# Filter taps of a state-space convolution from powers and weights instead of one exponential per state

## The reference

```python
def _L0_attn_a_ref(u, A_log, D, C_re, C_im, log_dt):
    dt = jnp.exp(log_dt)                      # one per channel m, 128
    A = -jnp.exp(A_log)                       # one per state n, 64
    t = jnp.arange(L_, dtype=u.dtype)         # 256 samples
    at = dt[:, None, None] * A[None, None, :] * t[None, :, None]
    K = jnp.einsum('mn,mln->ml', C_re, jnp.exp(at))
    u_f = jnp.fft.rfft(u.transpose(0, 2, 1), n=2 * L_)
    k_f = jnp.fft.rfft(K, n=2 * L_)
    y = jnp.fft.irfft(u_f * k_f, n=2 * L_)[..., :L_]
    return y.transpose(0, 2, 1) + u * D
```

## Time and profile before

| | before |
|---|---|
| median of 3 runs | 856.48 us (856.13 to 857.97) |
| the profiled execution | 855.01 us, of which the span of the instructions is 853.3 us |
| PE busy | 801.8 us, 94% of the span |
| ACT busy | 719.8 us, 84% |
| DVE busy | 682.4 us, 80% |
| POOL busy | 550.3 us, 64% |

### The profile page before, as it was taken

How to read it: one execution, slowest core, us unless ns; L and a number is a source line. 1 busy time by engine, 2 the same in 40 slices (tenths; PEclk the granted TensorE clock), 3 DMA queues, 4 the chain that set the end, 5 groups by cost and what they waited for, 6 DMA issues and landing times.

```text
span 853.3 us, 20661 instructions
## 1 busy us (share of the span) xinstructions
PE 801.8 (94%) x7793; PEld 446.1 (52%) x7793; DVE 682.4 (80%) x2000; ACT 719.8 (84%) x919; POOL 550.3 (64%) x620
## 2 busy tenths in 40 slices
PE   5899898989999999999999999999999999999995
PEld 4644475666677623333333333333333677777774
DVE  6898699999998766777777777778736899888884
ACT  7640488778888899999999999999998889999984
POOL 1187455535553498988899888888887555454542
PEclk9999999999999999999999999999999999999998
DMA  8201100000003334343334433433420000000000
GB/s 263 69 1 49 50 2 1 2 2 2 2 1 77 95 70 98 87 86 89 100 101 100 100 96 90 97 87 91 98 41 2 1 14 15 14 14 14 14 14 17
DMA packets 38521, 46.20 MB, mean 54 GB/s; under 512 B 6696, under 2 KB 24368, under 8 KB 38416
## 3 DMA queue, kind: packets, MB, share of 16 engines
q1 hardware_dynamic: 38416, 44.83, 20.8%
HBM read 28.03 MB, written 16.78 MB: 53 GB/s over the span
## 4 chain that ended last, share of the span: by engine, by line
PE 61%; ACT 14%; DVE 13%; issue 9%; POOL 3%; SPq 0%; DMA 0%; ACTq 0%
PE psum L816 16%; PE psum L762 15%; PE psum L1114 12%; ACT prob L1072 11%; PE psum L1063 5%; PE psum L1172 4%; DVE mixed L828 3%; DVE normed L351 2%; PE psum L566 2%; POOL prob L1087 2%; ACT decay L420 1%; PE psum L956 1%; PE psum L533 1%; PE psum L637 1%; DVE hidden_parts_first L785 1%
## 5 line engine op out<-in xcount | busy, mean ns | idle before, releaser
L1072 ACT ACTIVATE prob<-psum 128x1536 f32<-128x1536 f32 x256 | 347.7, 1500 | 15.5 <-PE psum L1063 15.5
L1114 PE MATMUL psum<-prob,vstack 128*32 128x256 f32 (+1 forms) x2048 | 204.9, 495 | 1.6 <-DVE o_tok L1122 1.6
L762 PE MATMUL psum<-xt_parts,w_parts 128*128 128x512 f16 x768 | 186.6, 379 | 0.0
L828 DVE SCALAR_TENSOR_TENSOR mixed<-psum,comb_y,mixed 128x128 f32<-128x128 f32 x512 | 143.1, 339 | 2.1 <-PE psum L816 2.1
L792 POOL TENSOR_TENSOR hidden_parts_second<-hidden_second,hidden_parts_second 128x512 f16<-128x512 f32 x64 | 78.9, 1233 | 91.8 <-ACT hidden_parts_second L778 91.8
L792 POOL TENSOR_TENSOR hidden_parts_first<-hidden_first,hidden_parts_first 128x512 f16<-128x512 f32 x64 | 77.9, 1222 | 77.7 <-ACT hidden_parts_first L778 77.5
L776 ACT ACTIVATE hidden_first<-psum,b 128x512 f32<-128x512 f32 x128 | 88.3, 690 | 29.1 <-PE psum L762 22.0
L1082 POOL TENSOR_SCALAR_AFFINE_SELECT prob<-prob 128x512 f32<-128x512 f32 x128 | 82.4, 644 | 41.0 <-ACT prob L1072 35.5
L1063 PE MATMUL psum<-qstack,kstack 32*128 32x512 f16 x768 | 99.7, 385 | 9.7 <-POOL prob L1087 4.8
L1063 PEld LDWEIGHTS psum<-qstack,kstack 32*128 32x128 f16 x768 | 24.9, 91 | 158.2 <-ACT prob L1072 139.8
L816 PE MATMUL psum<-w_parts,hidden_parts_first 128*128 128x128 f16 x1536 | 96.0, 219 | 10.5 <-DVE mixed L828 5.7
(11 more groups left out here) (121 smaller groups left out, 1101.1 us busy)
## 6 DMA issues: line engine op xcount, KB each, us to landing
qstack<-qk_parts SPq DMA_DIRECT2D x128, 128.0 KB, 3.6
qk_parts<-parts SPq DMA_DIRECT2D x64, 192.0 KB, 3.2
kstack<-qk_parts SPq DMA_DIRECT2D x128, 32.0 KB, 3.5
stream<-L_attn_a_u SPq DMA_DIRECT2D x4, 512.0 KB, 8.4
kept_x<-stream SPq DMA_DIRECT2D x4, 512.0 KB, 2.6
out<-mixed SPq DMA_DIRECT2D x8, 256.0 KB, 2.3
w_whole<-L_ffn_W SPq DMA_DIRECT2D x1, 1024.0 KB, 7.6
taps<-c_taps SPq DMA_DIRECT2D x1, 640.0 KB, 9.8
```

The lines of the kernel that those rows point to most:

```text
L762: last = e.matmul(bank(u % 4), m.w1[:, w_part, ex, cols], xt_parts[:, s, x_part, :], start=(n == 0), stop=(n == len(PRODUCTS) - 1))
L828: last = e.scalar_tensor_tensor(out=m.y[:, t0 + t, :], in0=bank(down_bank(m, i))[:, t * P:(t + 1) * P], scalar=comb_y[:, s, t, ex:ex + 1], ...
L1072: e.activation(prob[:, n % PROBS, :], psum[:, TILE * (n % 2):TILE * (n % 2 + 1)], ACT.Exp, scale=SCALE)\
L1114: last = e.matmul(to[SLOT * lane:SLOT * (lane + 1)], vstack[:, b % 2, keys, first:first + SLOT], weights_of(n - t, lane, keys, pair), star ...
```

## The change

Each exponential is split as t = 64 q + l, with four quarters q and 64 samples l: exp(z t) = exp(z l) * exp(z 64 q). Partitions are now two channels by 64 states, and 64 columns are the other 64 pairs of channels, so that `z` has one value for each of 128x64.

- The host lays `C_re`, `log_dt`, `A_log` and a ramp of 64 samples into one array `tap_cols` of 128x193, one transfer in place of four. `eye` and `skip_d` come later in the queue; `taps`, `inverse` and the chunks of the stream come ahead of `w1` and `w2`. Each has its own semaphore.
- ACT: four exponentials of 128x64, `leap`, for the quarters; five in place over `powers`, two of 128x512 and three of 128x1024.
- DVE: `grid` writes z * l into `powers` (pieces 0, 1, 2 and 4, TENSOR_TENSOR), and two products of 64x256 make `weight`, `leap` times the column of `C_re`, zero in the half of the other channel. POOL sets `weight` to zero and writes piece 3 of `powers`.
- PE: 32 fp32 products with `powers` (128x128) stationary and `weight` (128x16) moving. Each contracts over the 64 states. Half of what each gives is of use: `ktap_move` copies it to `ktap`, two copies by DVE and two by ACT. DVE adds `skip_d` to the first tap's row.
- Order: on PE the forward transforms 0 and 1 of chunk 0 stand behind the tap products, 2 and 3 behind the transform of the taps. On DVE the statistics of chunk 1 now stand behind `skip_d`.

```diff
-        for n in range(STATES):
-            if n >= ERING and n % 2:
-                e.wait_ge(chained, (n - ERING) // 2 + 1)
-            elif n >= ERING:
-                e.wait_ge(tapped, (n - ERING) // 2 + 1)
-            e.activation(decay[:, n % ERING, :], ramp[:], ACT.Exp, scale=z[:, n:n + 1]).then_inc(decayed, 1)
-        e.wait_ge(tapped, STATES // 2 + 2)
-        for h in range(HALVES):
-            last = e.copy(ktap[:, h, :], bank(6 + h)[:, 0:P])
+        for q in range(QUARTERS):
+            last = e.activation(leap[:, q, :], z[:], ACT.Exp, scale=float(QUARTER * q))
+        last.then_inc(leaped, 1)
+        for i, (lo, hi) in enumerate(GRIDS):
+            if i == GPSIMD_GRID:
+                e.wait_ge(gridded_too, 1)
+            else:
+                e.wait_ge(gridded, i + (i < GPSIMD_GRID))
+            piece = powers[:, lo:hi, :].rearrange("p n l -> p (n l)")
+            e.activation(piece, piece, ACT.Exp).then_inc(powered, 1)
+        e.wait_ge(tapped, 1)
+        for r in range(2):
+            last = e.copy(*ktap_move(1, r))
...
+    def grid(e, i):
+        lo, hi = GRIDS[i]
+        return e.tensor_tensor(powers[:, lo:hi, :],
+                               z[:, lo:hi].rearrange("p (n a) -> p n a", a=1).to_broadcast([P, hi - lo, QUARTER]),
+                               tap_ramp.rearrange("p (a l) -> p a l", a=1).to_broadcast([P, hi - lo, QUARTER]), ALU.mult)
+
+    def gpsimd_taps(e):
+        e.memset(weight[:], 0.0).then_inc(weight_zeroed, 1)
+        e.wait_ge(z_ready, 1)
+        grid(e, GPSIMD_GRID).then_inc(gridded_too, 1)
...
+        grid(e, 0).then_inc(gridded, 1)
+        grid(e, 1).then_inc(gridded, 1)
+        e.wait_ge(leaped, 1)
+        e.wait_ge(weight_zeroed, 1)
+        for j in range(2):
+            rows = slice(j * STATES, (j + 1) * STATES)
+            last = e.tensor_tensor(weight[rows, :, j, :], leap[rows].rearrange("p q n -> p n q"),
+                                   tap_cols[rows, 0:2 * GROUPS].rearrange("p (n a) -> p n a", a=1).to_broadcast(
+                                       [STATES, 2 * GROUPS, QUARTERS]), ALU.mult)
+        last.then_inc(weight_ready, 1)
+        grid(e, 2).then_inc(gridded, 1)
+        vector_conv_stats(e, 0)
+        grid(e, 4).then_inc(gridded, 1)
+        vector_conv_normed(e, 0)
+        e.wait_ge(tapped, 1)
+        for r in range(2):
+            last = e.tensor_copy(*ktap_move(0, r))
+        last.then_inc(ktap_moved, 1)
         e.wait_ge(s_small, SMALL)
...
+        e.wait_ge(ktap_moved, 1)
+        e.wait_ge(ktap_copied, 1)
+        e.tensor_tensor(ktap[0:1, 0, :], ktap[0:1, 0, :], skip_d[:], ALU.add).then_inc(skip_added, 1)
+        vector_conv_stats(e, 1)
...
+    def tensor_taps(e):
+        e.wait_ge(weight_ready, 1)
+        for g in range(GROUPS):
+            for i, (lo, _) in enumerate(GRIDS):
+                if lo == 2 * g:
+                    e.wait_ge(powered, i + 1)
+            last = e.matmul(bank(6)[:, 16 * g:16 * (g + 1)], powers[:, 2 * g:2 * (g + 1), :].rearrange("p s l -> p (s l)"),
+                            weight[:, 2 * g:2 * (g + 1)].rearrange("p s j q -> p (s j q)"), start=True, stop=True)
         last.then_inc(tapped, 1)
...
+        for pos in range(2):
+            tensor_forward(e, 0, pos)
+        e.wait_ge(s_taps, 16)
         e.wait_ge(skip_added, 1)
...
+        for pos in range(2, 4):
+            tensor_forward(e, 0, pos)
```

More of the change, by code:

```diff
@@ L29 @@
 BANK = 512
+QUARTER = 64
+QUARTERS = SEQ // QUARTER
+GROUPS = D // 4
+GRIDS = ((0, 8), (8, 16), (16, 32), (32, 48), (48, 64))
+GPSIMD_GRID = 3
 CONV_BATCHES = 4
@@ L176, in build_in @@
     with ExitStack() as own:
-        a_log, c_re = sb("a_log", [P, STATES], of=own), sb("c_re", [P, STATES], of=own)
-        log_dt, skip_d = sb("log_dt", [P, 1], of=own), sb("skip_d", [P, 1], of=own)
+        tap_cols = sb("tap_in", [P, 2 * 2 * GROUPS + QUARTER + 1], of=own)
+        skip_d = sb("skip_d", [1, D], of=own)
         forward = sb("forward", [P, HALVES, 4 * P], of=own)
@@ L184, in build_in @@
         b2_whole = sb("b2_whole", [COMB_ROWS, CH], of=own)
[L185 to L188, removed]
+        neg_a, dt, z = sb("neg_a", [P, 1], of=own), sb("dt", [P, 2 * GROUPS], of=own), sb("z", [P, 2 * GROUPS], of=own)
+        leap = sb("leap", [P, QUARTERS, 2 * GROUPS], of=own)
+        powers = sb("powers", [P, 2 * GROUPS, QUARTER], of=own)
+        weight = sb("weight", [P, 2 * GROUPS, 2, QUARTERS], of=own)
         ktap = sb("ktap", [P, HALVES, D], of=own)
@@ L429, in vector_taps @@
     def vector_taps(e):
         e.wait_ge(dt_ready, 1)
-        e.tensor_scalar(z[:], neg_a[:], dt[:, 0:1], -1.0, ALU.mult, ALU.mult).then_inc(z_ready, 1)
-        e.wait_ge(s_small, SMALL)
[L433 to L453, removed]
-                e.tensor_scalar(spread[:, r, :], eye[:], c_re[:, n:n + 1], None, ALU.mult).then_inc(spread_up, 1)
@@ L455, in vector_taps @@
-        e.wait_ge(chained, STATES // 2)
-        e.tensor_tensor(chain[:, 0, 0:1], chain[:, 0, 0:1], skip_d[:], ALU.add).then_inc(skip_added, 1)
-    def tensor_add_taps(e, rows, columns, first_of_all, final):
-        for h in range(HALVES):
-            last = e.matmul(bank(6 + h)[:, 0:P], rows[:, h * P:(h + 1) * P], columns, start=first_of_all, stop=final)
-        last.then_inc(tapped, 1)
[L463 to L467, removed]
-            if n % 2 == 0:
-                e.wait_ge(decayed, n + 1)
-                e.wait_ge(spread_up, n // 2 + 1)
-                tensor_add_taps(e, decay[:, n % ERING, :], spread[:, n % ERING, :], n == 0, False)
+        e.tensor_scalar(z[:], dt[:], neg_a[:, 0:1], -1.0, ALU.mult, ALU.mult).then_inc(z_ready, 1)
@@ L560, in tensor_inverse @@
     def tensor_inverse(e, ch):
+        if ch == 0:
+            e.wait_ge(s_inverse, 16)
         e.wait_ge(combined, 4 * (ch + 1))
```

67 lines of the change are left out of this document (36 added, 31 removed).

## The result

| | before | after |
|---|---|---|
| median | 857.23 us (4 runs, 856.13 to 858.32) | 846.16 us (4 runs, 845.95 to 846.79) |
| span of the profiled execution | 853.3 | 844.1 |
| products with `khat` begin | 41.88 | 31.22 |
| first activation of the mixture's hidden layer | 95.56 | 85.33 |

The ratio after to before is 0.9872, with a 95% interval of 0.9855 to 0.9889: faster by 11.1 us, 1.3%. Forecast were 846.8 and a range from 841.0 to 849.5.

A forecast was written before the change was run, and what follows sets the result against it. No engine was full until 41.88 us, as ring and sums made them wait in turn. The `khat` products would begin at 32.2, 9.7 us earlier, taking the median from 856.48 to 846.8 us, range 841.0 to 849.5.

The forecast's parts named there:

- Loads: Start of the kernel: `tap_cols`, now first in the queue, lands at 3.6 us (3.4 to 4.2); `z` ready at 4.3.
- DVE up to `weight`: DVE's first two `grid` pieces and two 64x256 products at 0.4 us each: `weight` ready at 8.7 us.
- The hold-up: POOL's piece of the powers makes a two-operand DVE instruction stand for up to 2.3 us before `weight`.
- PE: Tap products, 64 instructions: 13.4 us at TensorE's lower clock level or 6.4 at the upper; last ends at 22.1.
- the slower end: Tap products on PE: lower clock level for all 64 instructions, 0.21 us each, 13.4 us.
- Tail: Tap products to convolution: copies and `skip_d` 0.7 us, then DVE's statistics and norm with POOL's `rstd`, to 32.2.
- At worst in a tie: Before the `khat` products: DVE's chain ends last at 32.2 us, PE's transform of the taps at 28.4 to 31.9.
- Sum: Products with `khat` begin at 32.2 instead of 41.88 us; all 9.7 us reach the kernel's end, median 846.8.
- The clock's rise: TensorE's level rises within the tap products, 4.8 us earlier, 842.0; chance 0.26 with the hold-up, 0.08 without.
- No hold-up by POOL: POOL's piece doesn't delay DVE before `weight`: 2.3 us earlier, 844.5 with the clock low; chance 0.12.
- The transform of the taps as the bound: Level stays low through forward products and taps' transform; `khat` at 34.1, 7.8 us less than before, 848.7; chance 0.09.
- A level that stays low in the convolution: Gaps on PE drop the clock; convolution products cost 0.43 us more each, up to 42 us slower; chance 0.03.

The follow-up runs named there:

- e2: Kernel after the change, with piece 3 of the powers written by DVE behind piece 2 instead of by POOL: 845.14 us.
- e1: Kernel after the change, with 18 unread 128x512 fp16 products added on PE at the very start, ahead of the tap products: 843.47 us.
- e3: Kernel after the change, with 128 moving columns instead of 16 in the tap products, the extra results overwritten: 841.38 us.
- e5: Kernel after the change, with statistics and norm of chunk 1 on DVE ahead of its wait for the tap products: 843.40 us.
- e11: Kernel after the change, all powers pieces on DVE, new DVE order, transform of the taps ahead of all forward products, 16 moving columns, no added products: 843.57 us.
- e6: Kernel before the change, with 13 products of 128x512 fp16 added at the start of PE: 857.05 us against 856.97.
- e7: Kernel after the change, with both 18 unread products at the start of PE and 128 moving columns in the tap products: 841.05 us.
- e9: Kernel after the change, with tap_cols issued behind x chunk 0 instead of ahead of it: 849.90 us.
- e10: Kernel after the change, 128 moving columns, all powers pieces on DVE, new DVE order, transform of the taps ahead of all forward products, no added products: 838.15 us.

## Why the prediction was right

**Loads.** Landing 2.89 instead of 3.6: 2.1 us from the issue, shorter than the 2.6 of the nearest row. `z` was ready at 3.58 instead of 4.3.

**DVE up to `weight`.** The hold-up was there (e2). It was 1.8 us instead of 2.3, because DVE had 0.6 us of its own work while POOL's piece was already running. The products of 64x256 took 0.60 each instead of 0.4. Ready at 7.75 instead of 8.7, all but 0.25 of it from the landing.

**PE.** This was the choice on which the forecast hung, and the slower end was right: 0.214 per instruction from the first to the last, 13.84 us against 13.4. The last ended at 21.6, 22.1 was said. The reason given for the choice was weak, though, and here the prediction was lucky: it said only that the one rise in the trace came late, and gave the other choice a third of the chances. e1 and e3 give what was missing: in these runs the tap products as written neither raised the level nor kept it, and the same loads with 128 moving columns saw it rise in their midst.

**Tail.** Copies and `skip_d` 0.9 instead of 0.7, POOL's `rstd` with its handovers 2.1 instead of 2.65 (`vareps` took 0.25 us, not the 0.72 of the earlier trace rows), the rest as read. L564 at 31.2 instead of 32.2. That it would wait for DVE's statistics and not for `khat` was right. "At worst in a tie" was too careful: PE's forward products took 5.19, the level rose within them, and the transform of the taps ran at the upper one, so `khat` lay ready 1.9 us before. e5 took 2.1 us from the chain.

**Sum.** 9.7 us were forecast at L564, it was 10.66; the two larger errors of size, landing and `rstd`, went the same way, the tap products' 0.4 the other. That all of it would reach the end was right but for 0.4 us, which the convolution gave back between the landmarks. The traces show where. Before, the products waited 0.39 us for `khat`, and POOL's next `rstd` began 0.30 ahead of them; after, they don't wait, and it begins 0.17 behind them:

```profile
41.58 0.24 POOL L343 TENSOR_SCALAR vareps<-meanvar 128x8 f32<-128x8 f32 x1 [11.60 <-DVE meanvar L338]
...
31.39 0.24 POOL L350 TENSOR_SCALAR vareps<-meanvar 128x8 f32<-128x8 f32 x1 [4.49 <-DVE meanvar L345]
```

The norm behind the first products, which runs beside POOL, takes 5.41 us before and 5.85 after, and that is the 0.4. POOL's work moved by 41.58 - 31.39 = 10.19 us, the first hidden activation by 10.23: it is this that reached the end. That POOL's later start makes the norm longer is argued from these rows, not tested. The span fell by 9.2 and the median by 11.1, on both sides of it, which is the scatter of the attention and of what follows it: the attention took 364.7 us in the trace before, 365.3 in the one after. That the median came within 0.6 us of the forecast is thus in part luck.

**The rivals.** The clock's rise (842.0) didn't happen in the kernel after, and e3 has it, with 128 moving columns, and took 841.38. Its price was 4.8 us, and e3 gained 4.3 at the landmark and 4.8 in the median. No hold-up by POOL (844.5) was wrong, its price of 2.3 was 1.7. The transform of the taps as the bound (848.7) didn't come, since the level rose before it; e11 shows it, 4.61 us, once the transform comes first. A level that stays low in the convolution (slower than before) didn't come either. In the kernel after the gap in front of the next chunk's transforms was 0.8 us, and all 42 of them from 25.8 to 53.5 took 592 ns in the median, 667 at most. In e3, behind a wait of PE of 2.43 us, the level did fall, from 29.5 to 32.8 us (granted clock 0.50), and was up again behind it; it cost nothing that shows at the landmarks, 54.15 us apart against 54.11.

## What to carry to other kernels

When a change shortens the work of the engines around PE, ask what PE's instructions cost at the lower of its levels, and what fed PE until then: a cost that was hidden behind ACT's rows (0.2 us in e6, as far as it was tested) became one of 4.3 us (e3) to 5.5 us (e7) on the critical path. Cheap-looking products with few moving columns may be the dearest of the start, and widening them with columns that are thrown away can pay. Help from POOL has to be priced with what it holds up on DVE, and an input at the head of the queue was worth its landing time one to one here (e9), where the whole start hung on it.

## What the runs showed of the hardware

- A stream of 128x128 fp32 loads with 16 moving columns ran 13.84 us at the lower level without a rise. Begun at the upper level (e1) it fell to the lower at about 12 us, 1.6 us into unbroken work, and the granted clock read 0.50. With 128 moving columns the level rose at about 12 us (e3, e10), or was the upper one from 7.7 to 15.3 (e7).
- The granted clock of a stretch reads 1.00 at the start of a kernel although loads take 333 ns, and shows the lower level only once a change was recorded. The length of the loads, 333 or 192 ns, is the safer sign.
- A DVE instruction with two SBUF operands, started beside a POOL instruction of 2.40 us, took 2.39 us instead of 0.69, and ended 0.55 after it. The Trainium skill (GPSIMD Engine Reference, 1. Specifications) names the contention, and the trace agrees. In these rows it lasted until POOL's whole instruction was over, though DVE's first piece, begun 0.05 us ahead of POOL's, took its usual 0.69 beside it.
